# Layer 1 of a two-layer gated cross-attention kernel: products leave the short turn, and VectorE takes casts and some norms

## The reference

```python
def _rmsnorm(t):                                   # over the 8 numbers of one head
    return t * jax.lax.rsqrt(jnp.mean(t * t, axis=-1, keepdims=True) + 1e-6)
q = x @ Wq.T                                       # x: layer-normed tokens, 4 x 256 x 256
k, v = context @ Wk.T, context @ Wv.T              # context: 4 x 1601 x 256 (Wk, Wv interleaved)
q, k, v = heads(q), heads(k), heads(v)             # 32 heads of 8 numbers
q, k = _rmsnorm(q), _rmsnorm(k)
attn = jax.nn.softmax(jnp.einsum('bhnd,bhmd->bhnm', q, k) * 8 ** -0.5, axis=-1)
x = x + jnp.tanh(g_xattn[1]) * jnp.einsum('bhnm,bhmd->bhnd', attn, v)
x = x + jnp.tanh(g_ffn[1]) * (layernorm(x) @ weight.T + bias)
```

## Time and profile before

| | us |
|---|---|
| median of 3 runs | 1722.6 |
| the profiled execution | 1721.58 |
| its span in the trace | 1719.8 |
| layer 1's attention and last feed-forward in it | from about 1297 to the end |

### The profile page before, as it was taken

The page is one execution under the profiler, slowest core; times in us unless marked ns, Lnnn a source line. Parts: engine busy times, 40 slices in busy tenths (PEclk is TensorE's granted clock), DMA queues, the critical chain, the costliest instruction groups (busy, mean ns, idle before and its releaser), DMA issues. The chain is left out here.

```text
span 1719.8 us, 43340 instructions
## 1 busy us (share of the span) xinstructions
PE 1616.0 (94%) x16022; PEld 1011.1 (59%) x16022; DVE 1393.7 (81%) x3487; ACT 1381.0 (80%) x2317; POOL 1273.5 (74%) x1170
## 2 busy tenths in 40 slices
PE   3799999999999999999999999988998999999997
PEld 1466777767776677767777777766553333333332
DVE  8889999999999989999888888889995755555422
ACT  4688888788888788888888888873337999999996
POOL 3558778787787877887877787765896989989400
PEclk9899999999999999999999999998999999999998
DMA  4299989999999999999989999996323232222100
GB/s 175 87 177 203 195 206 205 195 205 222 202 189 200 190 198 185 224 211 207 196 194 218 217 194 209 211 186 175 104 44 108 44 77 39 44 39 45 26 14 14
DMA packets 608867, 261.07 MB, mean 152 GB/s; under 512 B 576528, under 2 KB 581648, under 8 KB 607248
## 3 DMA queue, kind: packets, MB, share of 16 engines
q1 hardware_dynamic: 604432, 258.05, 70.3%
q10 hardware_dynamic: 4224, 0.25, 0.2%
HBM read 99.15 MB, written 17.29 MB: 68 GB/s over the span
## 5 line engine op out<-in xcount | busy, mean ns | idle before, releaser
L1750 PE MATMUL pv<-PT,VV 128*128 128x256 bf16 (+1 forms) x2880 | 340.6, 275 | 12.1 <-DMA PT<-PB 12.1
L1730 PE MATMUL score<-KK,QT 128*128 128x512 bf16 (+2 forms) x1920 | 341.5, 322 | 6.5 <-DVE mxp L1225 6.5
L2316 POOL TENSOR_TENSOR l_rr<-l_rr,mhalf 128x32 f32<-128x32 f32 (+1 forms) x60 | 333.2, 5553 | 5.0
L1490 ACT ACTIVATE PB<-S,rsum 128x1024 bf16<-128x1024 f32 (+1 forms) x256 | 246.5, 988 | 106.0 <-DVE rsum L1256 81.6
L1750 PEld LDWEIGHTS pv<-PT,VV 128*128 128x128 bf16 (+1 forms) x2880 | 280.7, 99 | 79.9 <-issue 31.8
L1247 DVE SCALAR_TENSOR_TENSOR PB<-S,rsum,PB 128x1024 bf16<-128x1024 f32 (+1 forms) x256 | 297.6, 1163 | 3.1 <-ACT PB L1490 3.1
L1730 PEld LDWEIGHTS score<-KK,QT 128*128 128x128 bf16 x1920 | 158.1, 98 | 144.0 <-DVE mxp L1225 12.6
L1480 ACT ACTIVATE S<-S,nmx 128x1601 f32<-128x1601 f32 x128 | 210.2, 1643 | 7.2 <-DVE nmx L1237 7.0
L2582 ACT ACTIVATE P<-score 128x1024 f32<-128x1024 f32 x196 | 199.1, 1060 | 12.6 <-PE score L2674 5.9
L1068 POOL TENSOR_SCALAR S<-S,rsum 128x256 f32<-128x256 f32 x128 | 73.1, 571 | 129.8 <-DVE rsum L1256 116.2
L2694 PE MATMUL pv<-P,V 128*9 128x256 f32 (+1 forms) x2288 | 154.2, 384 | 3.8 <-DVE pv L2120 2.4
(11 more groups left out here) (264 smaller groups left out, 3577.6 us busy)
## 6 DMA issues: line engine op xcount, KB each, us to landing
x<-rs_d SPq DMA_DIRECT2D x16, 936.0 KB, 5.3
rsb<-rs_d SPq DMA_DIRECT2D x16, 936.0 KB, 5.5
wsb<-w_split SPq DMA_DIRECT2D x46, 256.0 KB, 4.7
wsb<-w_split SPq DMA_DIRECT2D x23, 512.0 KB, 4.9
wpr<-in_wprojT SPq DMA_DIRECT2D x23, 512.0 KB, 6.5
context_d<-stage SPq DMA_DIRECT2D x16, 400.2 KB, 3.7
l_ctx<-context_d SPq DMA_DIRECT2D x4, 1601.0 KB, 7.2
rawh<-in_w_all SPq DMA_DIRECT2D x12, 512.0 KB, 5.5
```

The source lines that it names most:

```text
L1490: e.activation(m.PB[n % 2][:, 2 * a:a + b], m.S32[n % 2][:, a:b], ACT.Copy, scale=m.rsum[n % 2][:, 1:2]).then_inc(s["p_hi"], 1)
L1730: i = e.matmul(m.score[:, at:at + b - a], qt[:, kind, qp, q * P:(q + 1) * P], kk[:, kp, a:b], start=(k == 0), stop=(k == 2))
L1750: i = e.matmul(m.pv[:, at:at + 256], vv[0:rows, v, t, :], m.PT[k % 2][0:rows, turned(c, a), :], start=(c == first and r == 0), stop=(c == ...
L2316: e.tensor_tensor(rr, rr, m.mhalf[0:rows, 0:NH1], ALU.pow).then_inc(s["l1_rr"], 1)
```

## The change

1. `product_turns` replaces the fixed turns. Whatever would fall in a short turn moves one turn later (`off_tail`). So an odd key chunk has "begin" in turn 5 and both "go_on" and "product" in turn 7. Token chunk 0 has its steps in turns 4 and 5 (before 3 and 4), token chunk 1 has both in turn 7 (before 6 and 7); their "turn_x" comes one turn later, in 3 and 6.
2. For batches 1 to 3 VectorE, not ACT, casts the turned tokens to their high part.
3. For chunks 7, 13 and 14 of batches 1 to 3 VectorE works out the inverse root itself, in 12 dependent small operations on 128x32 numbers (a first guess from integer operations on the upper 16 bits, and three Newton steps), in turns 30, 51 and 54. POOL leaves these out and its counters skip them. The stack steps of 13 and 14 come right behind in the same turns, 51 and 54 (before: 54 and 58).
4. In batch 3 the last two products of the feed-forward are in turns 11 and 12, not 12 and 13.

```diff
+OWN_NORMS = {7: 30, 13: 51, 14: 54}
+def off_tail(n):
+    return n + (n % L1U == L1U - 1)
+def product_turns(c):
+    if c < TB:
+        return ((4, 5), (7, 7))[c]
+    first = L1U * (c // 2) + (5 if c % 2 else 2)
+    return tuple(off_tail(first + i) for i in range(3))
 def l1_slots(n):
-        first = 3 + 3 * c if c < TB else L1U * (c // 2) + (5 if c % 2 else 2)
+        turns = product_turns(c)
-        if c < TB and n == first - 1:
+        if c < TB and n == turns[0] - 1:
             out.append(("turn_x", c))
-        if first <= n < first + len(parts):
-            out.append((parts[n - first], c))
-        if n == first + len(parts) + 4:
+        for part, turn in zip(parts, turns):
+            if n == turn:
+                out.append((part, c))
+        if n == OWN_NORMS.get(c, -1):
+            out.append(("norm", c))
+        if n == (OWN_NORMS[c] if c > 12 else turns[-1] + 5):
             out.append(("stack", c))
@@ pool_prepare
-    elif what == "product":
+    elif what == "product" and not own_norm(b, c):
+def dve_own_norm(e, m, s, k, rows):
+    e.wait_ge(s["l1_ss"], k + 1)
+    e.tensor_scalar(x, ss, 1.0 / D1, EPS6, ALU.mult, ALU.add)
+    e.tensor_scalar(bits(y), bits(x), 1, None, ALU.logical_shift_right)
+    e.tensor_scalar(bits(y), bits(y), -1.0, float(0x5F37), ALU.mult, ALU.add)
+    for i in range(3):                    # each of the 12 waits for the one before
+        e.scalar_tensor_tensor(a, y, -0.5, y, ALU.mult, ALU.mult)
+        e.tensor_tensor(a, a, x, ALU.mult)
+        e.scalar_tensor_tensor(y, a, 1.5, y, ALU.add, ALU.mult)
@@ dve_prepare, turn_x
+        if b:
+            e.wait_ge(s["xt_full"], TB * b + c + 1)
+            ...
+            e.tensor_copy(high part of l1_xT, x_bank(m, b)[:, 0:IC * P])
@@ last_turns
-    return tuple(2 * L1U * b + n for n in (2, 4, 10, 12, 13))
+    return tuple(2 * L1U * b + n for n in (2, 4, 10, 11, 12))
@@ act_prepare
-    if what == "turn_x":
+    if what == "turn_x" and b == 0:
```

More of the change, by code:

```diff
@@ L84 @@
 xst_done xmv_done xrs_eps xrs_done xn_done xt_full xT_hi xT_lo
-l1_pa l1_kn l1_sq l1_ss l1_rr0 l1_rr l1_pv0 praw_in   l1_v l1_hd l1_s0 stack_up
+l1_pa l1_kn l1_sq l1_ss l1_rr0 l1_rr l1_newton l1_pv0 praw_in   l1_v l1_hd l1_s0 stack_up
 stack_in0 stack_in1 l1_s l1_exp l1_pv l1_os l1_ot l1_den l1_att l1_added
@@ L257, in allocate @@
             m.l1_sq = sb(c, "l1_sq", [P, H], F32)
+            m.l1_nx = sb(c, "l1_nx", [P, NH1], F32)
+            m.l1_na = sb(c, "l1_na", [P, NH1], F32)
             m.l1_ss = [sb(c, f"l1_ss{i}", [P, NH1], F32) for i in range(3)]
@@ L2176, in l1_slots, with own_norm, pool_norms @@
     for c in range(L1C):
-        first = 3 + 3 * c if c < TB else L1U * (c // 2) + (5 if c % 2 else 2)
+        turns = product_turns(c)
         parts = ("begin", "product") if c < TB else PARTS
-        if c < TB and n == first - 1:
+        if c < TB and n == turns[0] - 1:
             out.append(("turn_x", c))
-        if first <= n < first + len(parts):
-            out.append((parts[n - first], c))
-        if n == first + len(parts) + 4:
+        for part, turn in zip(parts, turns):
[4 more added lines that the diff above has]
+        if n == (OWN_NORMS[c] if c > 12 else turns[-1] + 5):
             out.append(("stack", c))
     return out
+def own_norm(b, c):
+    return b > 0 and c in OWN_NORMS
+def pool_norms(k):
+    b, c = (k // L1C, k % L1C)
+    return k + 1 if b == 0 else k + 1 - len(OWN_NORMS) * (b - 1) - sum(c >= n for n in OWN_NORMS)
 def prepared(n):
@@ L2314, in pool_prepare @@
         e.tensor_scalar(rr, ss, 1.0 / D1, EPS6, ALU.mult, ALU.add).then_inc(s["l1_rr0"], 1)
-        e.wait_ge(s["l1_rr0"], k + 1)
+        e.wait_ge(s["l1_rr0"], pool_norms(k))
         e.tensor_tensor(rr, rr, m.mhalf[0:rows, 0:NH1], ALU.pow).then_inc(s["l1_rr"], 1)
@@ L2329, in pool_layer1 @@
     pool_last(e, m, s, B - 1)
+def dve_own_norm(e, m, s, k, rows):
+    x, y, a = m.l1_nx[0:rows, :], m.l1_rr[k % 3][0:rows, :], m.l1_na[0:rows, :]
+    bits = lambda t: t.bitcast(I16).rearrange("p (h w) -> p h w", w=2)[:, :, 1]
+    at = 12 * (k - pool_norms(k))
+    e.wait_ge(s["l1_ss"], k + 1)
+    e.tensor_scalar(x, m.l1_ss[k % 3][0:rows, :], 1.0 / D1, EPS6, ALU.mult, ALU.add).then_inc(s["l1_newton"], 1)
+    e.wait_ge(s["l1_newton"], at + 1)
+    e.tensor_scalar(bits(y), bits(x), 1, None, ALU.logical_shift_right).then_inc(s["l1_newton"], 1)
+    e.wait_ge(s["l1_newton"], at + 2)
+    e.tensor_scalar(bits(y), bits(y), -1.0, float(0x5F37), ALU.mult, ALU.add).then_inc(s["l1_newton"], 1)
+    for i in range(3):
+        e.wait_ge(s["l1_newton"], at + 3 * i + 3)
+        e.scalar_tensor_tensor(a, y, -0.5, y, ALU.mult, ALU.mult).then_inc(s["l1_newton"], 1)
+        e.wait_ge(s["l1_newton"], at + 3 * i + 4)
+        e.tensor_tensor(a, a, x, ALU.mult).then_inc(s["l1_newton"], 1)
+        e.wait_ge(s["l1_newton"], at + 3 * i + 5)
+        e.scalar_tensor_tensor(y, a, 1.5, y, ALU.add, ALU.mult).then_inc(s["l1_newton"], 1)
 def dve_prepare(e, m, s, b, what, c):
@@ L2354, in dve_prepare @@
     elif what == "turn_x":
+        if b:
+            e.wait_ge(s["xt_full"], TB * b + c + 1)
+            q = TB * b + c - 1
+            e.wait_ge(s["l1_pa"], place(q // TB, q % TB) + 1)
+            e.tensor_copy(m.l1_xT[:, 0, :, :].rearrange("p i t -> p (i t)"),
+                          x_bank(m, b)[:, 0:IC * P]).then_inc(s["xT_hi"], 1)
         e.wait_ge(s["xT_hi"], TB * b + c + 1)
@@ L2364, in dve_prepare @@
         if k >= 3:
-            e.wait_ge(s["l1_rr0"], k - 2)
+            e.wait_ge(s["l1_rr0"], pool_norms(k - 3))
         e.tensor_reduce(m.l1_ss[k % 3][0:rows, :], m.l1_sq[0:rows, :].rearrange("p (h d) -> p h d", d=D1),
                         AX.X, ALU.add).then_inc(s["l1_ss"], 1)
+    elif what == "norm" and b:
+        dve_own_norm(e, m, s, k, rows)
     elif what == "stack":
@@ L2374, in dve_prepare @@
             part = [st[0:rows, :, 0::2, :], st[0:rows, :, 1::2, :]]
-        e.wait_ge(s["l1_rr"], k + 1)
+        if not own_norm(b, c):
+            e.wait_ge(s["l1_rr"], pool_norms(k))
+        if own_norm(b, c):
+            e.wait_ge(s["l1_newton"], 12 * (k + 1 - pool_norms(k)))
         e.tensor_tensor(heads, heads, m.l1_rr[k % 3][0:rows, :].unsqueeze(2).broadcast_to([rows, NH1, D1]),
@@ L2558, in act_prepare @@
 def act_prepare(e, m, s, b, what, c):
-    if what == "turn_x":
[L2560 to L2563, removed]
+    if what == "turn_x" and b == 0:
+        e.wait_ge(s["xt_full"], c + 1)
+        if c:
+            e.wait_ge(s["l1_pa"], place(0, c - 1) + 1)
         e.copy(m.l1_xT[:, 0, :, :].rearrange("p i t -> p (i t)"), x_bank(m, b)[:, 0:IC * P]).then_inc(s["xT_hi"], 1)
```

## The result

| us | before | after |
|---|---|---|
| median of 6 runs each | 1721.34 | 1729.06 |
| span in the trace | 1719.8 | 1728.2 |
| layer 1's loop in the trace: first sums to last group copy | 404.30 | 411.38 |

The ratio is 1.0053, 95% interval 1.0038 to 1.0068. So the change makes the kernel slower, by 7.7 us where +3.2 was forecast (1725.8, with a range of its own from 1722 to 1730). Of the 8.4 us between the spans, 7.1 lie in the loop; the other 1.3 had gathered before it, in layers that the change doesn't touch.

The account below looks back on a forecast made before the run. In mid-batch PE and ACT were taken to share the bound, with further waits at batch starts. Terms -3.1 - 0.4 + 0.5 + 5.3 + 0.9 = +3.2 us gave 1725.8 (chance 0.45, own range 1722 to 1730; 8 in 10: 1713 to 1733).

Parts of the forecast that it names:

- the norm's price: VectorE's 12 chained operations on 128x32: 0.225 us from start to start, 2.7 us a norm, bounds 1.9 and 4.1.
- Rival (c): VectorE's norms are dear, operations costing 0.34 us like the reciprocal: +11.5 us, 1734.1; chance 0.11.
- the ledger: VectorE's list in turns 51 to 56, added up from stack 12 at 1497.63 to the group's copy starting at 1509.1.
- Rival (b): At the boundaries VectorE reaches the copy 3 us earlier than added up, nobody waits: -9.9 us, 1712.7; chance 0.11.
- the clock falls: Behind PE's boundary gaps the clock drops to 0.50 (1.2 GHz): 1.6 us at each of two boundaries, 1.0 at the third.
- Rival (a): The boundary stall is there but the clock stays: -1.0 us, 1721.6; chance 0.20.
- the late copy at full clock: At boundaries, PE's sums start 2.95 us late, 1.9 comes back: net +1.05 at the first two; -0.1 at the third.
- it is not earlier after the change: POOL's power of chunk 12 follows a root and chunk 11's power without a gap, so still ends at 1497.59.
- boundary 2 to 3: VectorE some 0.9 us earlier, shorter group gives 0.3, PE 1.75 late, DMA wait gone, 1.0 for the clock: +0.9.
- the merged products: Odd chunks leave PE's short turn in mid-batch: group 12.59 to 12.33 us, PE next limit, -3.1 us in all.
- Rival (d): Merged products give nothing: four product matmuls in a group's first turn delay scores, 3.1 us on top, 1728.9; chance 0.13.
- Norm 7 and the weights piece: Turn 30: the 2.7 us norm fits VectorE's idle, but in batch 0 a weights piece follows: +0.5 us, once.

Follow-up runs that it names:

- run 1: The changed kernel with chunk 14's norm and stack moved from turn 54 to 56, behind the group's copy in VectorE's list; 1715.15 us, 0.9967 of the kernel before.
- run 4: The changed kernel with 14 extra matmuls, results overwritten, at each of three batch boundaries to keep PE busy while it waits; 1724.64 us, 1.0019 of the kernel before.
- run 11: The changed kernel measured once more, unedited; 1728.95 us, 1.0039 of the kernel before, loop 411.83 us.
- run 5: The kernel before with only the three norms on VectorE in turns 30, 51 and 54, stacks of 13 and 14 in 51 and 54; 1731.44 us, ratio 1.0058.
- Run 6: The changed kernel with chunk 14's norm in turn 56, and chunks 3 and 11 also on VectorE; 1715.03 us, 0.9963 of the kernel before.
- run 7: The changed kernel with chunk 14's norm in turn 56, but the old product and token turns; 1720.49 us, 0.9988 of the kernel before.
- run 2: The changed kernel with chunk 14's norm back on GpSimd and its stack in turn 58; 1723.65 us, 1.0022 of the kernel before.
- run 3: The changed kernel with all norms back on GpSimd, merged products, VectorE's casts and last products kept; 1724.16 us, 1.0018 of the kernel before.

## Why the prediction was right in its mechanism and short in its size

- **Right: the norm's price.** The 12 operations start 0.21 to 0.23 apart, 0.17 to 0.19 long; from the first to the stack is 1503.60 to 1506.29, 2.69 us, where 2.7 was taken. Rival (c) is out. The Trainium skill, "VectorE: DVE Perf Modes", section on the TRN2 errata, has the formula with 151 cycles and one per element, an estimated 0.19 for 32 elements, and these rows bear it out; its table's 58 cycles (an estimated 0.09) they don't.
- **Right: the ledger.** From stack 12's start to the copy's start I added up 1497.63 to 1509.1, 11.5 us; it was 1502.07 to 1513.55, 11.48. PE's gap was 4.29 for 4.0, at 2 to 3 it was 3.21 for 3. Rival (b) needed a cheaper list. Its mechanism is run 1: nobody waits, and the loop gives -8.07 where -9.9 was worked out.
- **Right: the clock falls**, and costs 4.8 (after minus run 4; 5.1 by run 11) where I had 1.6 + 1.6 + 1.0 = 4.2. It lasted 6.8, 3.4 and 6.8 us rather than 3.4 each; the price per boundary was 1.60, 1.32 and 1.84. Rival (a) is out.
- **Wrong: the late copy at full clock**, predicted at 1.05 + 1.05 - 0.1 = 2.0, measured (run 4) at 2.17 + 2.30 + 1.31 = 5.8. The failed step is "it is not earlier after the change". That was true of chunk 12's power, but I took it to cost nothing, and wrote the gains of chunks 11 and 13 off as swallowed. PE's groups come earlier and the power does not, so it is later against them: stack 12 began 3.96 after the last copy (1493.67 to 1497.63) and begins 4.68 after it now. So the eighth group grew by 4.09 (12.07 to 16.16), of which my ledger gave 3.36 (copy at 1509.1, not 1505.74) and this step the rest. Run 5 is the test: there the groups are not shorter, and the eighth is 15.43. What came back in the next group, which I took at 1.9 on TensorE's side, was at most 1.9 from copy to copy (13.53 to 11.62, 13.39 to 11.61 in run 4), where by my terms it is 2.3 (1.9 and the 0.4 between 3.36 and 2.95).
- **Wrong above all: boundary 2 to 3.** I made VectorE 0.9 earlier there, as no root stands before the powers, and took off 0.3 for the shorter group. The 0.9 holds while the groups keep their length: in the kernel before and in run 5 stack 12 begins 3.04 after the last copy there. In the trace after, GpSimd is back to back in batch 2 as well (from 1573.90 on), the six groups there come out 1.59 shorter, and stack 12 begins 4.24 after the last copy, 1.20 later:
```profile
1600.49 0.42 DVE L2562 COPY l_O<-pv 128x256 f32<-128x256 f32 x1 [0.35 <-PE pv L2748]
...
1604.73 0.43 DVE L2431 TENSOR_TENSOR l_kn<-l_kn,l_rr 128x256 f32<-128x256 f32 x1 [0.83 <-POOL l_rr L2341]
...
1616.21 0.41 DVE L2562 COPY l_O<-pv 128x256 f32<-128x256 f32 x1
```
 The same 11.48 follows. This boundary cost 3.15 for 0.9, more than half of all that was missing (3.9); of the 3.15, 1.84 is the clock, for which I had 1.0.
- **Half right: the merged products.** 12.59 became 12.41 and not 12.33, since late next was not "PE itself" but GpSimd, which I had seen without a gap in batch 1 and did not ask for its period (6.20 twice). Run 6 gives PE's own floor, 12.26. In batch 0 the middle groups gained nothing (12.62 and 12.48, as before). That the sum outside the boundaries came out at -2.94 for -3.0 is in large part luck: the groups of chunks 11 and 13, not counted, changed by +0.05 to -0.33; batch 0's second group grew by 0.49 (13.92 to 14.41), as in every run with the new product turns and in none with the old; and batch 0's first group gave 0.87 for 0.4, but it gave 0.80 in run 5 too, without the casts and token steps to which I had put it down. Rival (d) is out, by run 7 plainly.
- **Small steps.** Norm 7 and the weights piece cost what was predicted: in run 5, where only the norms are new, the fifth group of batch 0, which has turn 30, takes 12.98 and not 12.31, +0.67 for +0.5; in batches 1 and 2, without the weights piece, it stays at 12.59. The way is the predicted one, TensorE's next chunk waits for VectorE's copy of the last, in the kernel after too:
```profile
1365.31 0.60 PE L2698 MATMUL pa<-l_w,l_ctx 128*128 128x512 bf16 x2 [0.71 <-DVE V L2609]
```
 There the merged turns hide most of it (12.44). The last products, counted as nothing, gave -0.5.
- **What stays open.** Loop +7.1, medians +7.7, and by run 11's ratio +6.7; the differences lie within the intervals. Not so in runs 1 to 4: their medians against the kernel before lie 2.3 to 3.5 us above what their loops say (-4.9 for -8.1 in run 1, +3.7 for +0.3 in run 2), and there is only one trace of the kernel before. Between the kernel after and run 1 ratios and loops agree (14.8 and 15.2 us). What decides whether the clock stays low for 3.4 or 6.8 us is open too: it was 3.4 and 6.8 behind the same gap in two traces of one kernel. That norm 13 could stand behind the copy as well was not tried.

## What to carry to other kernels

Work put on an engine's in-order list costs little by its own length and much by what stands behind it: here one norm and stack ahead of a copy cost 15 us of loop more than the same work right behind it. When a step shortens the groups of one engine, ask of every other engine for its period at the new pace: one that runs back to back does not come forward, and its results are late by most of the gain (here by 0.72 us for 0.81 in batch 1, by 1.20 for 1.59 in batch 2). Where a wait on TensorE of the size seen here can't be removed, count the clock apart from the wait; here it was nearly half of the boundaries' loss.

## What the runs showed of the hardware

- Stretches at 1.2 GHz lasted 3.4 or 6.8 us, behind gaps of 3.21 to 4.29 us alike: the 4.29 was followed by 3.4 in the kernel after and by 6.8 in run 11, the 3.21 by 6.8. A longer gap did not mean a longer penalty.
- Between about 1.5 and 2.5 us the length of a gap did not tell what followed. Behind 2.05 (run 5, boundary 2 to 3) and 2.44 (run 3, the same) the clock was at 0.50 for 3.4 us; behind 2.29 in the kernel before it stayed at 1.00, and behind 1.85 in run 2. In run 2 a gap of 1.49, 0.8 us behind one of 1.34, had 0.50 behind it for 6.8 us, and in run 3 one of 1.49 behind one of 0.41 for 3.4 us; but 1.50 behind 0.85 (run 2, boundary 0 to 1) left 1.00. Whether gaps add up was not tested.
- 3.19 us of matmuls in a gap of 4.35 (run 4) kept 1.00; three such fillings gave back 4.7 us of loop.
- The small VectorE operations cost the same on 65 partitions (0.18 to 0.19, 0.22 apart) as on 128, and on int16 every second half-word (0.19) the same as the two- and three-operand ones on float.
